# Six places for the second layer's weights and seven for the low rank's, taken from the DMA scratch, and two quadrants of x1 loaded one tile sooner

## The reference, cut to what matters

```
x = x + einsum('bsi,boi->bso', x, weight[ids0])        # weight: 8 matrices of 2048 x 2048
x = x + x @ W.T + b + (x @ A[ids1]) @ B[ids1] * 2.0     # A: 2048 x 16, B: 16 x 2048
```

## Time and profile before

| | |
|---|---|
| median of 3 executions | 2583.78 us (2579.9 to 2586.59) |
| the profiled execution | 2590.35 us, its span 2588.6 us |
| granted TensorE clock, mean | 0.998 |
| TensorE busy | 2558.9 us, 11232 matmuls |
| VectorE busy | 1683.2 us |
| ScalarE busy | 875.7 us |
| GpSimd busy | 1254.0 us |
| GpSimd's DMAs | 392.24 MB, 47.3% of 16 engines |
| SyncE's DMAs | 252.77 MB, 30.5% of 16 engines |

### The profile page before, as it was taken

How to read it: one execution, slowest core, us unless ns; L and a number is a source line. 1 busy time by engine, 2 the same in 40 slices (tenths; PEclk the granted TensorE clock), 3 DMA queues, 4 the chain that set the end, 5 groups by cost and what they waited for, 6 DMA issues and landing times.

```text
span 2588.6 us, 30986 instructions
## 1 busy us (share of the span) xinstructions
PE 2558.9 (99%) x11232; PEld 2109.1 (81%) x11232; DVE 1683.2 (65%) x1882; ACT 875.7 (34%) x1159; POOL 1254.0 (48%) x1470
## 2 busy tenths in 40 slices
PE   8999999999999999999999999999999999999998
PEld 7888888888888888888888788888888788888777
DVE  5455454464463364444533478899999778999997
ACT  4232242242242242322422333333333343333332
POOL 3434434444443344344323466656666665555565
PEclk9999999999999999999999999999999999999999
DMA  9889889999998898889968787445777955544675
GB/s 357 306 299 306 294 284 283 303 299 307 286 302 284 253 316 292 284 264 269 255 196 196 216 298 250 135 158 167 241 255 234 384 167 175 167 151 122 232 230 198
DMA packets 238955, 648.03 MB, mean 250 GB/s; under 512 B 30164, under 2 KB 46548, under 8 KB 238804
## 3 DMA queue, kind: packets, MB, share of 16 engines
q0 software_dynamic: 123168, 392.24, 47.3%
q1 hardware_dynamic: 115060, 252.77, 30.5%
q10 hardware_dynamic: 576, 1.05, 0.1%
HBM read 433.07 MB, written 212.86 MB: 250 GB/s over the span
## 4 chain that ended last, share of the span: by engine, by line
PE 92%; DMA 3%; DVE 3%; issue 1%; POOL 1%; ACT 0%; SPq 0%; DVEq 0%; ACTq 0%
PE bank L834 18%; PE bank L835 18%; PE bank L836 18%; PE bank L864 12%; PE bank L868 12%; PE bank L866 12%; DMA wl<-w1s 1%; PE bank L818 1%; PE bank L819 1%; DVE xc L732 1%; PE bank L882 1%; DMA bm<-bs 1%; DVE c L797 1%; POOL wl L414 1%; DVE c L795 0%
## 5 line engine op out<-in xcount | busy, mean ns | idle before, releaser
L414 POOL TENSOR_TENSOR wl<-wl 128x512 fp32r<-128x512 f32 x392 | 601.2, 1553 | 430.9 <-ACT wl L577 429.6
L834 PE MATMUL bank<-x_hi,w_hi 128*128 128x512 f32 x2048 | 797.7, 390 | 8.9 <-DVE w_lo L648 8.9
L835 PE MATMUL bank<-x_lo,w_hi 128*128 128x512 f32 x2048 | 797.4, 389 | 0.0
L836 PE MATMUL bank<-x_hi,w_lo 128*128 128x512 f32 x2048 | 797.4, 389 | 0.0
L864 PE MATMUL bank<-xc,wl 128*128 128x512 f32 x1568 | 613.2, 391 | 11.7 <-POOL wl L414 9.0
L868 PE MATMUL bank<-xc,wl 128*128 128x512 f32 x1568 | 611.2, 390 | 0.0
L866 PE MATMUL bank<-xc,wl 128*128 128x512 f32 x1568 | 611.2, 390 | 0.0
L531 ACT ACTIVATE w_hi<-w_raw 128x1024 fp32r<-128x1024 f32 (+1 forms) x258 | 258.0, 1046 | 971.6 <-PE bank L836 969.9
L753 DVE TENSOR_TENSOR x_raw<-bank,x_raw 128x512 f32<-128x512 f32 x128 | 88.5, 691 | 694.9 <-PE bank L836 644.5
L834 PEld LDWEIGHTS bank<-x_hi,w_hi 128*128 128x128 f32 x2048 | 384.9, 188 | 89.3 <-DVE w_lo L648 9.3
L836 PEld LDWEIGHTS bank<-x_hi,w_lo 128*128 128x128 f32 x2048 | 384.8, 188 | 80.1
(11 more groups left out here) (45 smaller groups left out, 1662.8 us busy)
## 6 DMA issues: line engine op xcount, KB each, us to landing
w_raw<-w0T SPq DMA_DIRECT2D x254, 512.0 KB, 8.0
wl<-w1s SPq DMA_DIRECT2D x392, 256.0 KB, 2.7
xss<-x_raw POOLq DMA_DIRECT2D x256, 256.0 KB, 4.5
w1s<-q_raw POOLq DMA_DIRECT2D x196, 256.0 KB, 7.3
q_raw<-w1T POOLq DMA_DIRECT2D x96, 512.0 KB, 9.7
xq<-xss POOLq DMA_DIRECT2D x40, 1024.0 KB, 7.1
x1s<-x_raw POOLq DMA_DIRECT2D x128, 256.0 KB, 2.9
c<-x1s POOLq DMA_DIRECT2D x32, 1024.0 KB, 8.1
```

Source lines behind the costliest of these rows:

```text
L414: pool.tensor_tensor(w[:, 1], w[:, 1].bitcast(F32), w[:, 0].bitcast(F32), ALU.subtract).then_inc(wl_ready, 1)
L834: pe.matmul(sums[s][:], w_hi[s][:, k, :], x_hi[:, k, :], start=(k == 0), stop=False)
L835: pe.matmul(sums[s][:], w_hi[s][:, k, :], x_lo[:, k, :], start=False, stop=False)
L836: mm = pe.matmul(sums[s][:], w_lo[s][:, k, :], x_hi[:, k, :], start=False, stop=(k == KT - 1))
```

## The change

`WL` becomes 6 and `BM` 7. The new places lie behind c1 in the second layer's memory, past all that the first layer uses. For this the scratch of GpSimd's DMAs shrinks from 8192 to 2048 bytes of each partition. The first low-rank blocks and the first hm are loaded behind the weights of tile 2 * WL = 12 instead of tile 5. In the first layer GpSimd loads the quadrants xq1 and xq3 behind the stores of tile TILES - 3 instead of TILES - 2, with the wait that their memory is free; xq2 stays where it was.

```
-    WL = 5
-    BM = 3
+    WL = 6
+    BM = 7
...
-            wl = [sb2(f"wl{i}", [P, 2, Q, P], F32R) for i in range(WL)]
+            wl = [sb2(f"wl{i}", [P, 2, Q, P], F32R) for i in range(5)]
...
-            bm = [sb2(f"bm{i}", [P, P], F32R) for i in range(BM)]
+            bm = [sb2(f"bm{i}", [P, P], F32R) for i in range(3)]
...
             c1 = sb2("c1", [P, 4, Q, TOK])
+            bm += [sb2(f"bm{i}", [P, P], F32R) for i in range(3, BM)]
+            wl += [sb2(f"wl{i}", [P, 2, Q, P], F32R) for i in range(5, WL)]
...
-                    if n == WL:
+                    if n == 2 * WL:
                         sp.wait_ge(b_stored, NB * 2 * 16)
                         for i in range(BM):
                             load_bm(i)
...
-                    if n == TILES - 2:
+                    if n == TILES - 3:
                         pool.wait_ge(w_ready, w_total(TILES))
                         load_xq(0, 1)
                         load_xq(0, 3)
+                    if n == TILES - 2:
                         pool.wait_ge(tile_done, TILES - 1)
                         load_xq(0, 2)
...
-    nc = bacc.Bacc("TRN2", target_bir_lowering=False, num_devices=1, dynamic_dma_scratch_size=8192)
+    nc = bacc.Bacc("TRN2", target_bir_lowering=False, num_devices=1, dynamic_dma_scratch_size=2048)
```

## The result

The changed kernel takes 2575.16 us (median of 7 runs, 2573.94 to 2578.44), the kernel before 2584.97 us (7 runs beside them, 2579.9 to 2588.14). The ratio is 0.9966, 95% interval [0.9956, 0.9976]: 9.8 us by the medians, 6 to 11 by the interval. The forecast was 2578.8, 5.0 us saved. The time lies in the range; that it is faster by more than 0.3% had a chance of 0.38, less than "the same" had.

A forecast was written before the change was run, and what follows sets the result against it. TensorE, with work in 99% of the span, was taken as the bound, with about 14 us to win. Seam -6.3, blocks -2.3 and group's change +3.6 gave -5.0 us: median 2578.8 us, range 2567 to 2590.

The forecast's parts named there:

- The price (place 3): Change of batch group, 2000 to 2075: smaller scratch holds GpSimd's DMAs; holes 8.7 us instead of 5.1, 3.6 us lost.
- The fourth waits for the oldest to land: GpSimd's bursts at the group's change: 2048 bytes of scratch hold three large DMAs, so the next is held.
- the hole of the seam's kind: Group's change: TensorE waits 4.6 us for tile 198's weights, which GpSimd makes late after the held c loads.
- the slow clock: Group's change: lower clock behind the 4.6 us hole, expected to cost 2.8 to 3.1 us, taken as 2.8.
- (a): Rival: the scratch never holds GpSimd; the group's change gives back 5.1 us instead of costing; 2570.1 us, chance 0.33.
- (b): Rival: only two large DMAs fit; longer holds in three bursts from 2024 on; 2602 us, chance 0.15.
- The seam (place 1): Between the layers, near 1478 to 1488: sixth weight place and earlier quadrants remove hole and slow clock, gain 6.3 us.
- has 4 us to spare: Seam: c block lands at about 1472.5, so VectorE's chain to releasing tile 8 has this slack.
- rival (c): Seam: the c load comes no sooner because accumulating stores hold the queue; 3.5 of 6.3 us lost; 2582.3 us, chance 0.14.
- With six places: Seam: tile 6's weight load goes out at 1464.4 instead of 1467.57, missing by 0.1 us only even if no faster.
- The blocks (place 2): Low-rank matmuls from 1529 and near 2403 and 2484: seven places remove waits for block loads, gain 2.3 us.
- VectorE is late there, and no edit touches its work: Other holes, like 1700 to 1750 with four matmuls missing, were put down to VectorE and counted as not winnable.

The follow-up runs named there:

- second profile of before: The kernel before, unchanged, profiled once more: 2584.46 us, ratio 0.9997; the profiled execution's span was 2579.1 us.
- experiment 3: Kernel before with scratch 4096 and one part alone: six weight places 2580.15 us; seven low-rank blocks, first filled at the tenth tile of weights, 2581.18 us.
- experiment 2: Changed kernel, one part undone: five weight places 2582.73 us; three blocks 2583.72, with scratch 4096 2577.55; quadrants back at TILES - 2 2580.76.

## Why the prediction was right or wrong

**The price (place 3): right in mechanism and place, and in size as a sum.** "The fourth waits for the oldest to land" is what the timeline shows: three fit. Forecast were 8.7 us of holes, measured 8.1, partly by luck: the hole of the seam's kind is 3.6 instead of 4.6, the slow clock 1.7 instead of 2.8, the rest 2.8 instead of 1.3. Against the two profiles of before (5.8 and 2.8) the loss is 2.3 or 5.3; forecast 3.6. The scratch alone cost 4.9, and 6.2 beside six places, three blocks and the early quadrants (2048 against 4096). Rivals (a), no hold, and (b), two fit, fall. One sign was named wrongly: the DMA instructions keep their 0.77 us, and the hold is idle time ahead of them. I said that all of them staying at 0.77 would mean (a); a reader of durations alone would have concluded just that. I also named holds in the first layer as a sign of (b). In the first layer the holds are there (30.9 us ahead of q_raw's loads, L389, in the changed kernel) and cost TensorE nothing, as the price's paragraph said; as a sign of (b) they mislead, since three fit:

```profile
L389 POOL DMA_DIRECT2D q_raw<-w1T x96 | 51.1, 540 | 31.3 <-issue 30.9
```

**The seam (place 1): 4.4 us instead of 6.3** (5.4 against the second profile of before). The weights and the clock went as forecast. The step that failed is that the c block's chain "has 4 us to spare". The block landed at 1474.95, not 1472.5: 3.8 us sooner than before instead of 6.3, so that rival (c), by which it comes no sooner, has a part of the truth. And the first tile behind its chain is not tile 8 but tile 7: ScalarE's copy of tile 7's weights (1480.10 in the chain) stands in program order behind its first half of the new term, and TensorE wants that tile 2.72 us sooner. The way from the landing to the released tile took 8.1 us (1474.95 to 1483.06), where I had 7.0 for tile 8 (1478.8 to 1485.8). So 4 - 2.45 - 2.72 - 1.1 is 2.3 us late, and TensorE shows 2.0. The first profile of before had it all: there tile 7 starts at 1486.95, 8.2 us after the block's landing and 0.4 us late. It is 8.1 to 8.2 us in all nine profiles in which this chain is what tile 7 waits for. That the c load is what was left is shown by loading it first: 0.5.

The seam's gain was also put down to the wrong part. "With six places" the weights' wait goes, and it does; but in experiment 3 the sixth place alone leaves 8.2 us and the seven blocks alone 7.3, both behind the c block, and in experiment 2 the early quadrants with five places leave 3.8. What brought the seam down is that the c block lands sooner, and that came with the early quadrants (7.1 us without them).

**The blocks (place 2): under-sized.** 2.3 us counted; the holes of the rest of the second layer are 4.9 us in the second profile of before and 5.9 to 7.1 in the other four with three blocks, and 0 to 0.4 in those with seven blocks and six places. Seven places alone brought 3.8 us. My sum took the places where I saw a block as releaser and left the smaller holes near other low-rank products (1608, 1845, 1926, 2252, 2332: 1.4 us in the first profile) to VectorE; with them it would have been 3.7. Behind the other parts of the change they are worth more: 8.6 us in experiment 2. Its profile has 7.1 us of holes in the rest, 1.1 more at the group's change and 1.7 more at the seam. The seam's are a slow clock: the hole ahead of tile 7 is 2.0 us instead of 1.8, and behind it the granted clock reads 0.57 from 1484 to 1488, where the changed kernel's reads 1.00. Why the rest has 7.1 us of holes here and 4.9 in the second profile of before isn't shown.

**"VectorE is late there, and no edit touches its work": wrong as a reading.** I took one profile's small holes for the kernel's. They were that execution's, 6.6 us above the median that I had; a second one had none of them. The one near 1880 came again in two others with five places (0.5 and 0.9 us) and in none of the eight with six, so a small part of them may be the sixth place's; that isn't shown. The forecast for the median was spared the error only because I subtracted differences from the median, not because I knew.

**The tail: not counted.** From the last matmul to the end stand 6.5 to 8.4 us in the five profiles with five places and 4.8 in all eight with six. The last two yT stores of 1024 KB stand on GpSimd ahead of the weights; the sixth place lets GpSimd be a tile further. In the changed kernel they go out at 2558.7, 8.8 us before the last matmul at 2567.5; in the first profile of before at 2574.2, 6.1 us before 2580.3. The difference of 2.7 us is one tile. That this is the cause is argued from the order, and shown only in so far as the sixth place alone brings it. It is worth 1.7 to 3.6 us against the two profiles of before.

**The sum.** By the stretches, against the first profile of before and the second: seam -4.4 and -5.4, rest of the layer -10.2 and -4.9, group +2.3 and +5.3, tail -3.6 and -1.7. With the start's (+0.3, -0.2) this is -15.6 and -6.9, the spans' 16.3 and 6.8; the medians' 9.8 lies between. By the experiments: sixth place -4.8, blocks -3.8, quadrants -5.6, scratch +4.9, together -9.3. That this comes near 9.8 is luck, since the parts don't add: taken out of the changed kernel, sixth place, blocks and quadrants are worth 7.6, 8.6 and 5.6. Against the forecast of -5.0, the blocks brought 1.5 to 2.6 us more and the tail 1.7 to 3.6 more, the seam 0.9 to 1.9 less, and the group's change lies to either side. The range of 2567 to 2590 was wide enough for these errors; the likeliest class (no change beyond 0.3%) did not hold.

## What to carry to other kernels

Ask of a buffer that is taken from GpSimd's DMA scratch how many large DMAs are on the way at the worst moment; look for holds in the idle time ahead of the DMA instructions, not in their length. When a kernel loses a few microseconds in many small holes, take a second profile before giving a hole to an engine: here one execution's holes differed by 7 us from another's of the same kernel. And when one wait is removed, follow each engine's program order to the first tile that stands behind the next one: the spare time counts from that tile.

## What the runs showed of the hardware

In the second layer each held DMA of 1024 KB went out 0.31 to 0.32 us after the landing of an older one. The most of them (each in 512 pieces) that the profiles show on the way at once, the newest included, are three with 2048 bytes, five with 3072, and with 4096 seven, with no hold; there the seventh was issued 0.3 us before the oldest landed. An estimate from these runs alone: the fourth doesn't fit in 2048 bytes nor the sixth in 3072, so each takes over 512 bytes of a partition's scratch, and seven in 4096 leave it 585 at most.

The Trainium skill, "DMA: Bandwidth & Descriptors", has 16 bytes to a descriptor (section "Terms"), and eight and a closing one on each engine for 1 MiB in 128 pieces (section "The descriptor swizzle"). The prediction's estimate from them is 33 descriptors in a ring for our 512 pieces, 528 bytes, hence 128 / 33, 192 / 33 and 256 / 33, three, five and seven. The traces agree at all three sizes; that the eighth would wait at 4096 no run here shows.
